# A new fixed order of products on TensorE for a 12-step cycle, and bias copies directly behind their bank's last exponential, in a graph attention kernel

## The reference

```python
h = maximum(layernorm(x), 0);  x = x + relu(((D^-1/2 (adj + I) D^-1/2) @ h) @ weight)
h = maximum(layernorm(x), 0)
q = (h @ Wq.T).reshape(d, n, 8); k, v = likewise            # d = 128, n = 3327
a = einsum('dnh,dmh->dnm', q, k) * d ** -0.5 + adj + adj
out = einsum('dnm,dmh->dnh', softmax(a, axis=2), v)
x = x + out.reshape(n, 8 * d) @ Wo.T
```

## Time and profile before

| | us |
|---|---|
| median of 3 runs (lowest, highest) | 14540.83 (14539.84, 14545.1) |
| the profiled execution, its own time | 14539.52 |
| its span, first to last instruction | 14537.5 |
| mean granted TensorE clock, share of full | 0.988 |
| VectorE busy | 13807.0 |
| TensorE busy | 13815.3 |
| ScalarE busy | 13448.6 |
| sweeps | 13312 |
| exponentials | 26624 |

### The profile page before, as it was taken

One profiled execution on the slowest core, in us unless ns is written; L12 is line 12 of the kernel. 1 busy time (PEld: TensorE's weight loads), 2 busy tenths in 40 slices (PEclk: granted clock), 3 DMA queues, 4 the chain that ended last, 5 costly groups with the idle time before them and its releaser, 6 DMA issues. The chain is left out here.

```text
span 14537.5 us, 430687 instructions
## 1 busy us (share of the span) xinstructions
PE 13815.3 (95%) x143755; PEld 4900.9 (34%) x143755; DVE 13807.0 (95%) x27589; ACT 13448.6 (93%) x30466; POOL 327.4 (2%) x945
## 2 busy tenths in 40 slices
PE   3889999999999999999999999999999999999997
PEld 2533333333333333333333333333333333333333
DVE  4589999999999999999999999999999999999992
ACT  1269999999999999999999999999999999999996
POOL 1100000000000000000000000000000000000000
PEclk7989999999999999999999999999999999999999
DMA  8975655656565565656566565656556565555653
GB/s 274 258 161 135 144 135 136 142 133 140 136 143 135 137 141 134 141 134 144 134 137 141 133 142 134 143 135 136 142 134 142 133 144 135 139 138 134 144 132 83
DMA packets 2075308, 2084.40 MB, mean 143 GB/s; under 512 B 818905, under 2 KB 1827808, under 8 KB 2066752
## 3 DMA queue, kind: packets, MB, share of 16 engines
q1 hardware_dynamic: 2044590, 2035.44, 58.7%
q10 hardware_dynamic: 28560, 21.27, 0.5%
HBM read 1922.23 MB, written 133.76 MB: 141 GB/s over the span
## 5 line engine op out<-in xcount | busy, mean ns | idle before, releaser
L235 DVE CUSTOM_DVE_ANT_0 X<-X,adj_row 128x832 f32<-128x832 f32 x13312 | 13316.2, 1048 | 109.4 <-PE X L257 71.5
L997 ACT ACTIVATE prob<-S 128x416 f32<-128x416 f32 x26624 | 11895.3, 517 | 270.4 <-PE S L1067 88.2
L1067 PE MATMUL S<-q_blk,k_res 52*128 52x416 f16 x26624 | 6859.3, 343 | 50.0 <-ACT S L986 16.5
L1088 PE MATMUL O<-prob,v_pad 128*32 128x208 f32 (+1 forms) x87376 | 6721.0, 388 | 2.6
L257 PE MATMUL X<-mk,mq 40*128 40x416 f16 x26624 | 6270.6, 344 | 297.5 <-DVE m_part L235 271.1
L1067 PEld LDWEIGHTS S<-q_blk,k_res 52*128 52x128 f16 x26624 | 2217.6, 93 | 4255.5 <-ACT S L986 1451.8
L1088 PEld LDWEIGHTS O<-prob,v_pad 128*32 128x32 f32 x87376 | 1829.8, 108 | 2534.7 <-issue 2051.4
L257 PEld LDWEIGHTS X<-mk,mq 40*128 40x128 f16 x26624 | 1583.8, 93 | 2360.9 <-DVE m_part L235 1910.1
L235 DVE DVE_READ_ACCUMULATOR2_ANT m_part<- 128x1 f32 x13312 | 1893.3, 142 | 0.0
L986 ACT ACTIVATE S<-adj_key 128x416 f32<-128x416 f32 x3328 | 1752.4, 527 | 58.6 <-issue 23.2
L207 POOL TENSOR_SCALAR m_neg<-m_full 128x16 f32<-128x16 f32 x208 | 52.6, 253 | 13062.4 <-DVE m_full L218 13062.2
(11 more groups left out here) (86 smaller groups left out, 1044.5 us busy)
## 6 DMA issues: line engine op xcount, KB each, us to landing
adj_key<-adj_by_key SPq DMA_DIRECT2D x3328, 208.0 KB, 3.4
adj_row<-in_adj SPq DMA_DIRECT2D x1200, 416.0 KB, 3.8
mk<-k_planes SPq DMA_DIRECT2D x1664, 104.0 KB
adj_row<-adj_tail SPq DMA_DIRECT2D x400, 416.0 KB, 3.9
mk<-k_planes SPq DMA_DIRECT2D x1664, 52.0 KB
row<-in_adj SPq DMA_DIRECT2D x47, 1663.5 KB, 8.3
adj_by_key<-aT SPq DMA_DIRECT2D x26, 1664.0 KB, 11.7
q_planes<-q_parts SPq DMA_DIRECT2D x26, 1024.0 KB, 15.0
```

What stands on the lines that cost most here:

```text
L235: nc.vector.tensor_tensor_reduce(out=x_, in0=x_, in1=adj_row[gi % 4][:].rearrange("p (a b) -> p a b", a=2), scale=1.0, scalar=LOW, op0=ALU ...
L997: nc.scalar.activation(prob[c % QR][:, d % 4, :], S[b][:, 0:WB], ACT.Exp, scale=2.0).then_inc(s_e[b], 1)
L1067: nc.tensor.matmul(S[b][:, 0:WB], k_res[base:base + KR, d // 2, s * P:(s + 1) * P], q_blk[n % 2][base:base + KR, d // 2, :], start=False, ...
L1088: done = nc.tensor.matmul(O[32 * d:32 * d + 32, cols], v_pad[:, s, 4 * q + d, :], prob[born(j, q) % QR][:, d, cols], start=first, stop=Tru ...
```

## The change

The order of letters in a cycle is another one, given as one string; `FULL` says the same as before. `LATER` becomes 0 for all banks. `cycle` numbers fills, units and halves by counting letters instead of by steps. The counts per cycle are the same for fills, `x`, `y` and halves; there are 10 `v` and 1 `V` where there were 8 `v` and 2 `V`.

```diff
-    ORDER = ("xy01v", "0xy1v", "0x1y", "x0y1v", "x01yv", "v0xy1v", "x01y", "0vxy1", "0xy1v", "0xy1V", "0xy1", "0xyV1")
-    FULL = ("0xy1", "0xy1V") * 6
+    ORDER = "vxy01xy0v10xy1vx0y1vx01yV0xy1xy0v1x01yvx0y1vx01yvvx01yvxy01"
+    FULL = "0xy10xy1V" * 6
     HELD = 14
     FIRST = 24
-    LATER = (1, 0, 1)
+    LATER = (0, 0, 0)
@@
-                    for letter in "".join(ORDER):
+                    for letter in ORDER:
@@
-                            half = 12 * c - HELD
-                            for i, step in enumerate(order):
-                                p = 12 * c + i
-                                for letter in step:
-                                    if letter in "01":
-                                        scores(k, 2 * p + int(letter), end // 4)
-                                    elif letter in "xy":
-                                        maximum(pe, k, LEAD + p, 1 if letter == "x" else 0, end)
-                                    else:
-                                        wide = 2 if letter == "V" else 1
-                                        if half < end:
-                                            values(k, half, wide)
-                                        half += wide
+                            half, fill, unit = 12 * c - HELD, 24 * c, 2 * (LEAD + 12 * c)
+                            for letter in order:
+                                if letter in "01":
+                                    scores(k, fill, end // 4)
+                                    fill += 1
+                                elif letter in "xy":
+                                    maximum(pe, k, unit // 2, 1 - unit % 2, end)
+                                    unit += 1
+                                else:
+                                    wide = 2 if letter == "V" else 1
+                                    if half < end:
+                                        values(k, half, wide)
+                                    half += wide
```

## The result

The kernel after takes 14,687.2 us in the median (14,671.3 to 14,702.8, 4 runs) against 14,543.0 (4 runs): 1.0101 times as long, 95% interval 1.0089 to 1.0113. The profiled execution took 14,682.0, its span 14,680.0. Forecast were 14,636 and slower.

What follows compares the result with a forecast made beforehand. VectorE's sweeps were taken as largest, with TensorE and ScalarE near, tied by waits in a quiet cycle of 12.08 us. Sum: 14,539.5 + 55 (small operations) + 47 - 6 (output copies) = 14,636 us; range 14,505 to 14,720.

Steps and rivals of the forecast that it cites:

- signs of being wrong: Quiet cycle off 12.08 us by over .03, no wait at h10, or granted clock falling outside the loop boundaries.
- (a): ScalarE: two bias copies come one exponential earlier, costing .28 us per cycle, covered by spare time; the wait at W1 goes.
- (c): TensorE's path to sweep W5: it starts at 6.08 us where six free sweeps need 5.89, so .19 is lost.
- (d): TensorE's path to sweep W10: it starts at 11.10 us against 10.98 free, .12 lost; quiet cycle again 12.08.
- The bound (+.09 for each such x): On TensorE each x that waits may hold its partner another .09 us: +.09 x 1,050 = +95.
- (e): VectorE's reduce and transpose, once in 64 sweeps, pass on .37 us per 64 sweeps against .09: +55 us.
- (f): Output copy on ScalarE: h10, now adjacent to h9, waits for it, 1.41 us; +1.12 x 42 = +47 us.
- The -6 for the copy behind h5: Output copies at h5 and h1 have scores between still; their .2 may shrink at h5: -6 us.
- FULL: Of the 1,094 cycles, 42 run FULL, which was said to stay.
- The clock: Rival: the new wait at h10 lets the granted clock fall, 42 x 3.9 = +164 us, some 14,800; chance .03.
- The faster rival's condition: y5 starts by 5.51 instead of 5.71, so sweeps run at VectorE's pace: 14,451 us, half lead 14,516; chance .20.
- TensorE obey its order strictly: Premise from the rows on TensorE: its operations run strictly in program order, with fixed start intervals between slots.

Runs made afterwards that it cites:

- run 3: The kernel before with only LATER set to (0, 0, 0), so old order with immediate bias copies: 14,710 us, 1.0113 times before.
- Run 4: The kernel after with the V of h4 and h5 taken apart into two single v: 14,694 us, 1.0104 times before.
- run 8: The kernel after with F18 placed ahead of x9 and F19 behind it: 14,609 us, 1.0055 times before.
- run 5: The kernel after with the output copy behind h9 one exponential earlier in ScalarE's order: 14,663 us, 1.0086 times before.
- run 1: The kernel after with h10 moved behind x10 F20 F21 y10: 14,649 us, 1.0074 times before.
- run 2: The kernel after with the bias copies of before, LATER = (1, 0, 1): 15,054 us, 1.035 times before.
- run 6: The kernel after with every cycle in ORDER, so no FULL cycle: 14,633 us, 1.0063 times before.

## Why the prediction was right or wrong

Direction, range and the two places of the waits were right; +144 us was measured for +96 forecast. Two of the prediction's own signs of being wrong came all the same: the quiet cycle is .075 off 12.08, and once the granted clock fell in a cycle far from any loop boundary. By its steps:

- **(a) LATER.** Right that ScalarE's spare time covers .28 and that W1's wait goes. It missed that the gain is one of the pair only: run 3 shows the same copies lengthening the path to W1 in the old order.
- **(c) Path to W5.** Right to .01: from x1 to W5 4.93 forecast, 4.94 measured. Run 4 shows the V in it.
- **(d) Path to W10.** Wrong in size: .12 forecast, .18 measured. I gave the .08 behind a waiting x to x7, where it did not occur, and took x8 and x9 as not waiting. x9 did wait for W7, and F18 and y9 were .083 late. The bound (+.09 for each such x) held it; run 8 shows that it is this term. With .01 more at W5 it makes the .075 per ordinary cycle, the +62 us of the account, where I had a quiet cycle unchanged.
- **(e) The small VectorE operations.** Wrong: +55 us forecast, nearly nothing measured. The mean of ordinary cycles lies .019 over their median after, .021 before. One of them lengthens the distance of two sweeps by .16 to .18, not by its .24 to .255, and the later waits swallow most of that.
- **(f) The output copy.** Right: 1.41 forecast for the cycle, 1.34 measured (13.49 against 12.155). The successor loses .02 instead of the .21 of before (put at .29), so the copy costs 1.15 x 42 = 48 us, where +47 was forecast. The table's 61 less 2 hold beside it 6 of the loss that these 84 cycles share with the ordinary ones, and the 5 of the clock's fall. Runs 5 and 1 show it. The -6 for the copy behind h5 was +3.
- **FULL** was said to stay; it cost +25 us. Its letters stayed, but not what stands around them. Median distances of sweeps in the cycle that ran FULL (for run 2 the length is that of the 20 cycles named above):

| kernel | FULL cycle | W1 to W2 | W9 to W10 | W11 to the next W0 |
|---|---|---|---|---|
| before | 12.68 | 1.12 | 1.24 | 1.12 |
| run 3: old order, immediate copies | 12.94 | 1.41 | 1.12 | 1.20 |
| run 2: new order, copies of before | 13.04 | 1.12 | 1.24 | 1.47 |
| after | 13.29 | 1.40 | 1.12 | 1.55 |

The immediate copies make .25 of the .61 in either order, at the same sweeps. The other .35 comes with the new order, at the seam: its cycle begins with a lone `v`, which now stands directly behind the last `V` of FULL, and x0 starts 1.19 after that `V` instead of .84. It is gone where FULL is (run 6); moving that `v` alone was not tried. After, then before:

```profile
5726.16 1.26 PE L1088 MATMUL O<-prob,v_pad 128*32 128x416 f32 x16
5727.35 0.35 PE L257 MATMUL X<-mk,mq 40*128 40x416 f16 x2
...
5727.85 1.03 DVE L235 CUSTOM_DVE_ANT_0 X<-X,adj_row 128x832 f32<-128x832 f32 x1 [0.43 <-PE X L257]
```

```profile
5675.35 0.91 PE L1088 MATMUL O<-prob,v_pad 128*32 128x416 f32 x8
5676.19 0.35 PE L257 MATMUL X<-mk,mq 40*128 40x416 f16 x2
```

- **The clock** was a rival with .03, for every copy behind h9. It struck one of the 42, at 5 us where 3.9 a time were reckoned. The Trainium skill ("TensorE: Matmul & The Clock Gate", What's actually happening) says that idleness brings back the half clock; here the half clock followed one of these 42 waits, and in run 2 it followed 20 of 42 waits of 1.08 us.

So (d) and (e) failed in opposite directions by about 60 us each; that they nearly cancel is luck, and the sum looks better than its terms. The faster rival's condition, y5 started by 5.51, was not met (5.71 forecast, x1 at .20 and y5 at 4.76 measured, so 5.71 in the same count).

## What to carry to other kernels

In a hand-made order on an engine that takes its work in that order, each letter has a release and a deadline; walk them all, in the cycle and in the rare cycles too (block boundaries, special orders), for a loss that is removed at one place comes back at the next deadline. The seam counts too: a special cycle that keeps its letters gets longer when its neighbour begins with another letter. A product that may have to wait is better placed behind its partner than ahead of it, where the delay of the partner reaches a deadline (run 8). Two changes that only work together, as an order and the place of the copies that feed it, must be judged together.

## What the runs showed of the hardware

- On TensorE the score behind an x that waited, on other array rows, started .083 later than the x at x9 (in nine of ten ordinary cycles), and within .003 of it at x7 and x8 of the same cycle, though all three x had waited for some .04. I did not find the condition, and could not have forecast which x it strikes.
- A dependent ScalarE instruction directly behind its source starts .54 to .58 after it (the bias copies in the kernel after, .57 in the median), an independent one .40 to .41.
- A VectorE operation of .24 to .255 between two sweeps lengthens their distance by .16 to .18 only.
- The prediction had TensorE obey its order strictly. Between the two groups of array rows it did not always: in the cycle of after that starts at 6410.74, F14 starts at 6417.03 and x7, ahead of it in the program on the other rows, at 6417.07.
- A wait of TensorE of 1.08 to 1.20 us was followed by the half clock in 20 of 42 cases in run 2 and in one of 42 in after. Its length alone does not decide it: 42 waits of 1.18 to 1.25 in run 8 left the clock at 1.00.
